# Seven PSUM banks in one ring for self attention, in place of a ring of four and a ring of three

## What is computed

```python
q = (x @ Wq.T).reshape(Bv, Tv, H, D).transpose(0, 2, 1, 3)
k = (x @ Wk.T).reshape(Bv, Tv, H, D).transpose(0, 2, 1, 3)
v = (x @ Wv.T).reshape(Bv, Tv, H, D).transpose(0, 2, 1, 3)
scores = jnp.einsum('bhqd,bhkd->bhqk', q, k) / scale
bias = -dist[None, :, :] * slopes[:, None, None]
bias = jnp.where(causal_mask[None, :, :], -jnp.inf, bias)
attn = jax.nn.softmax(scores + bias[None], axis=-1)
out = jnp.einsum('bhqk,bhkd->bhqd', attn, v)
return out.transpose(0, 2, 1, 3).reshape(Bv, Tv, D_MODEL) @ Wo.T
```

## Time and profile before

| | |
|---|---|
| median of 3 runs | 2000.3 us (1983.67 to 2005.92) |
| profiled execution, its own time | 2008.43 us |
| its span | 2006.6 us |
| mean granted TensorE clock | 0.918 |
| PE / DVE / ACT / POOL busy | 1847.0 / 1292.4 / 921.7 / 973.4 us |
| stretch of self attention | 0 to some 696 us of the span |

### The profile page before, as it was taken

One profiled execution on the slowest core, in us unless ns is written; L12 is line 12 of the kernel. 1 busy time (PEld: TensorE's weight loads), 2 busy tenths in 40 slices (PEclk: granted clock), 3 DMA queues, 4 the chain that ended last, 5 costly groups with the idle time before them and its releaser, 6 DMA issues.

```text
span 2006.6 us, 29476 instructions
## 1 busy us (share of the span) xinstructions
PE 1847.0 (92%) x10650; PEld 927.7 (46%) x10650; DVE 1292.4 (64%) x2503; ACT 921.7 (46%) x1866; POOL 973.4 (49%) x824
## 2 busy tenths in 40 slices
PE   7888999999999899999999999999999999999962
PEld 3444444444444464454554554554454554554431
DVE  4567666775652255776665665665665665668998
ACT  2235556664654424334445445445445445445441
POOL 1000000000000046666888888888888888882244
PEclk9759888997877779999999999999999999999985
DMA  4332022213001100000000000000000000000001
GB/s 104 39 35 34 1 34 34 34 12 83 1 2 53 32 10 1 1 1 10 4 1 10 4 1 10 4 1 10 4 2 10 4 1 1 4 10 22 1 22 42
DMA packets 28744, 34.46 MB, mean 17 GB/s; under 512 B 4098, under 2 KB 26947, under 8 KB 26947
## 3 DMA queue, kind: packets, MB, share of 16 engines
q1 hardware_dynamic: 28600, 32.59, 9.0%
HBM read 14.99 MB, written 4.19 MB: 10 GB/s over the span
## 4 chain that ended last, share of the span: by engine, by line
PE 74%; DVE 14%; ACT 6%; issue 3%; SPq 2%; DMA 1%; POOL 1%; POOLq 0%; ACTq 0%; DVEq 0%
PE psum L951 16%; PE psum L931 13%; PE psum L916 9%; PE psum L836 8%; DVE maxima L1216 6%; PE psum L750 5%; PE psum L811 5%; PE psum L784 4%; ACT weights_room L1034 3%; PE psum L904 3%; PE psum L974 3%; PE psum L848 2%; PE psum L962 2%; DVE parts_room L1310 1%; PE psum L820 1%
## 5 line engine op out<-in xcount | busy, mean ns | idle before, releaser
L1216 DVE TENSOR_REDUCE maxima<-psum 128x1 f32<-128x400 f32 (+5 forms) x1664 | 860.3, 579 | 359.1 <-PE psum L916 208.6
L725 POOL TENSOR_TENSOR parts_room<-parts_room,weights_room 128x512 f32<-128x512 f32 (+1 forms) x565 | 705.3, 1281 | 136.5 <-ACT weights_room L1106 136.5
L1106 ACT ACTIVATE weights_room<-psum 128x512 f32<-128x512 f32 (+1 forms) x757 | 406.5, 600 | 493.8 <-PE psum L931 419.3
L1034 ACT ACTIVATE weights_room<-psum 128x512 f32<-128x512 f32 (+3 forms) x640 | 298.3, 536 | 252.4 <-PE psum L811 128.5
L1423 POOL TENSOR_SCALAR rstd<-meanvar 128x2 f32<-128x2 f32 (+1 forms) x24 | 8.2, 343 | 731.6 <-DVE meanvar L1166 731.6
L931 PE MATMUL psum<-stack_room,dk_hi 64*128 64x512 f32 (+1 forms) x1408 | 261.8, 407 | 7.2 <-ACT weights_room L1106 7.1
L916 PE MATMUL psum<-k_later,stack_room 64*128 64x400 f32 (+1 forms) x896 | 242.4, 410 | 22.4 <-DVE stack_room L1266 14.6
L811 PE MATMUL psum<-stack_room,stack_room 51*128 51x512 f32 (+3 forms) x640 | 208.7, 467 | 26.4 <-ACT weights_room L1034 23.8
L916 PEld LDWEIGHTS psum<-k_later,stack_room 64*128 64x128 f32 x896 | 128.0, 183 | 220.8 <-issue 121.1
L951 PE MATMUL psum<-weights_room,late_room 128*64 128x512 f32 (+1 forms) x760 | 205.5, 612 | 0.0
L951 PE MATMUL psum<-weights_room,parts_room 128*64 128x512 f32 (+1 forms) x754 | 202.3, 604 | 0.0
(11 more groups left out here) (133 smaller groups left out, 1959.7 us busy)
## 6 DMA issues: line engine op xcount, KB each, us to landing
stack_room<-parts_room SPq DMA_DIRECT2D x96, 128.0 KB
x_block<-x_dram SPq DMA_DIRECT2D x8, 512.0 KB, 4.9
x_middle<-x_block SPq DMA_DIRECT2D x4, 512.0 KB, 3.1
x_block<-x_middle SPq DMA_DIRECT2D x4, 512.0 KB, 3.9
out_dram<-x_block SPq DMA_DIRECT2D x8, 256.0 KB, 2.1
parts_room<-ctx_dram SPq DMA_DIRECT2D x1, 1536.0 KB
stack_room<-shift_rows SPq DMA_DIRECT2D x64, 2.0 KB
parts_room<-wq_dram SPq DMA_DIRECT2D x8, 128.0 KB, 2.2
```

What stands on the lines that cost most here:

```text
L725: engine.tensor_tensor(sum_[:kw, :], old[:kw, :], weights[u % NP_WEIGHTS][:kw, :], ALU.add) \
L1034: engine.activation(w_self[s % NW][:, m, 0:n], self_scores[(HP * s + m) % SELF_SCORES][:, 0:n], ACT.Exp, scale=SELF_SCALE).then_inc(exp_do ...
L1106: engine.activation(weights[u % NP_WEIGHTS][:kw, :], pair_scores[u % NSCORES][:kw, :], ACT.Exp, scale=CROSS_SCALE).then_inc(pair_exp, 1)
L1216: engine.tensor_reduce(maxima[:, p % 2, i // TB, n, i % TB, ch:ch + 1], bank_of(use + n)[:, 0:real - k0], AX.X, ALU.max) \
```

## The change

The ring of three is dropped. `SELF_RING` becomes 7, a scores stage puts down two uses of the common ring, and takes both banks ahead of its first matmul, as a chunk stage does. The counters `scored` and `exp_done` are replaced by `bank_full` and `bank_free` of the banks concerned. A bank is now reused after seven uses of whatever kind. Cross attention's rings stay.

```diff
-SELF_RING, SELF_SCORES = 4, 3
+
+SELF_RING = 7
...
-            self.put("scores", p, b, j, self.step)
+            self.put("scores", p, b, j, self.step, banks=HP)
...
+    def scores_made(s):
+
+        return bank_filled(scores_use[s] + HP - 1)
+
+    def weights_made(s):
+
+        return bank_read(scores_use[s] + HP - 1)
...
-    self_scores = [psum[:, SELF_RING + i, :] for i in range(SELF_SCORES)]
...
+                slots = [take_bank(use + m) for m in range(HP)]
                 for m in range(HP):
                     r = slice(m * HALF, m * HALF + USED)
-                    u = HP * s + m
-                    if u >= SELF_SCORES:
-                        pe.wait_ge(exp_done, u - SELF_SCORES + 1)
-                    last = engine.matmul(self_scores[u % SELF_SCORES][:, 0:n],
+                    last = engine.matmul(slots[m][:, 0:n],
                                          k_stack[p % NSTACK][r, j * P:(j + 1) * P], q_stack[p % NSTACK][r, q0:q0 + n],
                                          start=True, stop=j < TB * b)
                     if j < TB * b:
-                        last.then_inc(scored, 1)
+                        filled(use + m, last)
...
-                pe.wait_ge(exp_done, HP * (s0 + 2))
+                pe.wait_ge(*weights_made(s0 + 1))
...
-                    act.wait_ge(scored, HP * s + m + 1)
-                    engine.activation(w_self[s % NW][:, m, 0:n], self_scores[(HP * s + m) % SELF_SCORES][:, 0:n],
-                                      ACT.Exp, scale=SELF_SCALE).then_inc(exp_done, 1)
+                    act.wait_ge(*bank_filled(use + m))
+                    engine.activation(w_self[s % NW][:, m, 0:n], bank_of(use + m)[:, 0:n],
+                                      ACT.Exp, scale=SELF_SCALE).then_inc(emptied(use + m), 1)
```

More of the change, by code:

```diff
@@ L483, in _decoder @@
     scores_at = [s.at for s in stages if s.kind == "scores"]
+    scores_use = [s.use for s in stages if s.kind == "scores"]
     pair_scores_at = [s.at for s in stages if s.kind == "pair_scores"]
@@ L515, in _decoder @@
     stored = [sem(f"stored{i}") for i in range(2)]
-    scored, exp_done, values_done = sem("scored"), sem("exp_done"), sem("values_done")
+    values_done = sem("values_done")
     shift_ready = sem("shift_ready")
@@ L819, in tensor_program @@
                             r = slice(m * HALF, (m + 1) * HALF)
-                            last = engine.matmul(self_scores[(HP * s + m) % SELF_SCORES][:, 0:P], halves[r, half, :],
+                            last = engine.matmul(slots[m][:, 0:P], halves[r, half, :],
                                                  mask_cols[r, half, :], start=False, stop=half == 1)
                             if half:
-                                last.then_inc(scored, 1)
+                                filled(use + m, last)
             elif kind == "values":
@@ L873, in tensor_program @@
                     pe.wait_ge(*bank_read(CROSS_USE - n))
-                pe.wait_ge(exp_done, HP * SELF_STEPS)
                 pe.wait_ge(raw_made, len(finish_no))
@@ L1068, in scalar_program @@
                 else:
-                    act.wait_ge(scored, SELF_STEPS)
+                    act.wait_ge(*scores_made(SELF_STEPS - 1))
                     act.wait_ge(values_done, SELF_STEPS)
@@ L1256, in vector_program @@
                 statistics(TB * b, TB, lambda t: x_blocks[b % 2][:, t, :])
-                dve.wait_ge(scored, HP * (last_step(NP - NSTACK, NB - 1) + 1))
+                dve.wait_ge(*scores_made(last_step(NP - NSTACK, NB - 1)))
                 normalise(stats_of["self_norm", b], resid[:, tiles(b), :], x_blocks[b % 2], b)
@@ L1518, in sync_program @@
                 if p >= NSTACK:
-                    sp.wait_ge(scored, HP * (last_step(p - NSTACK, NB - 1) + 1))
+                    sp.wait_ge(*scores_made(last_step(p - NSTACK, NB - 1)))
                 for m in range(HP):
```

## The result

The changed kernel took 1942.8 us (median of 4 runs, 1940.27 to 1943.58) against 1998.9 us of the kernel before beside it: a ratio of 0.974, 95% interval 0.970 to 0.978. In a later set of runs it was 0.976 (0.971 to 0.980). So 56 us were won where 36 were forecast.

What follows compares the result with a forecast made beforehand. TensorE was taken to bound the kernel, busy 92% of the span, so only its waits or clock could be won. Terms of 10 + 14 + 12 = 36 us gave 1964 us from a median of 2000.3; range 1922 to 2000 us.

Steps and rivals of the forecast that it cites:

- The wait changes its name: Full groups: the second scores step waits for VectorE's maximum instead of ScalarE's exponential, gaining 0.04 us of 2.83 us.
- The 0.15 us behind a wait for two banks: Second scores step: its matmuls start 0.15 us, not 0.05 us, after the awaited bank is free.
- Groups with a rows stage: Four places per head pair: second scores step also needs the first chunk's second reduce; -0.56 us each.
- Pairs 1 to 6: Head pairs 1 to 6: comparison of bank releases with scores starts gave +14 us net, taken as 10 us.
- Pair 7: Last head pair, without maxima: scores have seven banks nearly alone; 14 us gain, bounds 11 and 17.
- Pair 0 and the start: First stretches: scores gain 7.5 us, chunks waiting for maxima 4.5; together 12 us, bounds 4 and 20.
- The bounds: Whole kernel: the ends of the terms were said to give 2004 us and 1913 us.
- the granted clock should be as before in each stretch: Expected in the profile after: TensorE's clock unchanged in every stretch, so the gain comes from waits.
- the prediction's own sign: Whole kernel: the prediction is wrong if head pairs get longer or the clock column moves by more than 0.05.
- the rival: Self attention: denser work gives back a third of 227 us at half speed, 38 us more, 1926 us; chance 0.17.
- More waits at a step's head: Scores steps wait for two semaphores at their head: cost nothing; 10 us if 0.03 us a step.
- VectorE as a brake: Rival, pairs 1 to 6: late VectorE reduces hold up scores; 41 us slower, 2041 us; chance 0.14.

Runs made afterwards that it cites:

- split take: The changed kernel, but each scores matmul waits for its own bank just ahead of it, not for both at the step's head: 1925.6 us, later 1919.7 us.

## Why the prediction was right, and where not

**The wait changes its name.** Right: 1.37 us and 2.80 us a group were computed, and read. The 0.15 us behind a wait for two banks, on which this rests, was right as well. The pulled-ahead weight load of the Trainium skill (TensorE: Matmul & The Clock Gate, "Step-by-step: what each phase is for") is not seen at these waits. The load of a waiting matmul starts only behind the event: in the split take, with one bank to wait for, 0.05 us behind it (331.24 against 331.19). The split take shows what one wait per matmul is worth, 0.09 us a group.

**Groups with a rows stage.** The second step there does wait for both reduces: in pair 3 its group's chunk starts at 337.76 and the step at 339.75, 1.99 us behind, where 1.82 + 0.15 were expected (0.53 us to the first reduce, then 0.69 and 0.60 us, and the 0.15 us):

```profile
337.76 0.50 PE L793 MATMUL psum<-stack_room,stack_room 51*128 51x512 f32 x2
...
339.75 0.50 PE L818 MATMUL psum<-stack_room,stack_room 51*128 51x512 f32 x2 [0.51 <-DVE maxima L1222]
340.19 1.08 PE L855 MATMUL psum<-fold,o_raw 128*128 128x34 f32 x8
```

The same place in the kernel before:

```profile
360.21 0.50 PE L784 MATMUL psum<-stack_room,stack_room 51*128 51x512 f32 x2
...
362.45 1.08 PE L848 MATMUL psum<-fold,o_raw 128*128 128x34 f32 x8
```

From chunk to fold it takes 2.43 us where it took 2.24. The loss is 0.19 us and not 0.56, since the same group was held up before too, at its second chunk.

**Pairs 1 to 6.** 10 us by the waits in the two profiles, as the sum had it; the old wait put back there cost 15 us at equal clock. The term was about right or too small, and it holds a loss that the sum did not have, the 3 us of pair 5. **Pair 7.** 10 to 12 us by the waits (the table of the profiles, and the wait put back), for 14: a term too large by a quarter. Folds are one reason: in this pair TensorE waits 5.9 us for the copy ahead of a fold, where it waited 0.7 us before. **Pair 0 and the start.** 5 us for 12: the term that was mis-sized most. VectorE is busy for 77 us of the 97 us; that its throughput, not its banks, made most of those waits is my reading, and no run shows it. **The bounds** of the terms were added up wrongly: -14, +11 and +4 are a gain of 1 us, not a loss of 4.

**The step that failed** is "the granted clock should be as before in each stretch". It rose by 0.27 in pair 7 and by up to 0.1 elsewhere, and gave 42 us in the two profiles, some 19 us over all executions. By the prediction's own sign (wrong if the clock column moves by more than 0.05) its mechanism was incomplete. I had this as a rival with 0.17 and 38 us more. The waits gave 25 to 32 us of the forecast 36. The direction held on its merits; that the measured 1942.8 us lies in the range is owed to the rival, whose time, and not the terms of the forecast, set the lower end at 1922. Pairs 1 to 4 got 2 to 7 us shorter, not 1 to 3, and pair 7 took 66 to 73 us, not 86. The argument against the rival, that the fall in pair 3 comes behind diagonal tiles and a fold, which stay, was half right: the fall stays, but is shorter (7 us for 10). The Trainium skill (TensorE: Matmul & The Clock Gate, "A second HAM failure mode: psum-queue depth-cycling") ties a swinging clock to short idles between groups of matmuls. In pair 7 the traces agree: with a stall of 0.85 us in a group of 2.6 us the clock is 0.72, filled it is 0.96. In pairs 3 and 4 with the old wait put back they do not: more stall, and a clock of 1.00.

**More waits at a step's head** cost nothing to be seen; **VectorE as a brake** was refuted as the outcome and confirmed as a mechanism, above.

**What stays open.** Why the clock stayed up in pairs 3 and 4 when the old wait was put back there, and why pair 0 gets anything from 0.57 to 0.72 with the same instructions. The runs show that filled stalls keep the clock up; they don't give a rule by which a single fall could be foretold. The price of a microsecond of half clock is not one number: 0.26 to 0.41 us in single stretches, 0.32 us over all executions. No run here issues the shifts' transfer ahead of the cross-attention loads, which might save the 6 us of pair 5.

## What to carry to other kernels

Where TensorE's clock swings, a stall of TensorE can cost its own length and about as much again, or its length alone: one wait put back in pair 7 cost 12 us of stall and 16 us of clock, in pairs 1 to 6 it cost 15 us and no clock. So forecast both, and before you trust a split made from two profiles, look how the clock of the profiled executions lies among the others. Before banks are pooled, write down which use each step will now wait for, since a common ring ties a step to whatever reads slowest seven uses back, a transfer in another queue included (pair 5); and take each bank just ahead of the matmul that needs it. If a stall can't be removed, two useless matmuls in each may pay for themselves, as in the kernel before; in the split take they did not.

## What the hardware showed that I had not expected

Work that leaves the result unchanged made the kernel faster: 280 repeated matmuls brought 1% (0.990), by raising the granted clock of pairs 1 to 4 from 0.85 to 0.92 up to 0.97 to 1.00. A microsecond at half speed costs 0.26 to 0.41 us in single stretches and 0.32 us over all executions; if TensorE's clock alone set the pace it would be 0.5, since half of the time would be saved. And the clock has a large spread of its own between executions: in profiles in which pair 0's instructions and waits were the same, its clock was 0.57 to 0.72 and its length 97 to 107 us, which is as much as many of the effects measured here.
